# Expert matmuls in two column halves, the second one with weights as stationary operand

## The chip, the cores and the metric

The kernel runs on one core of a Trainium2 chip. The metric is device time in microseconds (us) of one execution. A core has TensorE (PE, matmul; PEld is its weight load), VectorE (DVE), ScalarE (ACT), GpSimd (POOL), SyncE (SP, which here only issues transfers) and 16 DMA engines. TensorE reads from SBUF and writes to PSUM, whose banks VectorE and ScalarE empty.

## The reference

A small vision tower on 32 images of 3x96x96: 36 tokens per image, 1152 tokens of 128 features. It makes shifted patch tokens, a rotary attention block with a feed-forward net, a lower-triangular token mix, a differential attention block, and last a block with attention and a mixture of 64 experts. The change touches the experts only:

```python
ef = gate_i.reshape(-1)              # two experts of 64 for each token
pos = ...                            # place of the token in its expert's list
keep = (pos < C)                     # C = 2 * (T * 2 // E) = 72 slots
buf = jnp.zeros((E, C, H)).at[ef, posc].add(tok)
h = jax.nn.gelu(jnp.einsum('ech,ehf->ecf', buf, w1) + b1[:, None, :])
y = jnp.einsum('ecf,efh->ech', h, w2) + b2[:, None, :]
ys = y[ef, posc] * (gf * keep)[:, None]
return x + ys.reshape(T, TOP_K, H).sum(axis=1)
```

Here E is 64, C is 72, H is 128 and F is 512, so each expert has two weight matrices of 128x512 and 512x128 float32, 512 KB together.

## The kernel before

The first two thirds of the program are the blocks ahead of the experts; their order on each engine is a table written out by hand (ORDERS_FOUND), and nothing of it changes. The tokens are then written to a table of slots in HBM (`slot_rows`), and from there come back as `xrows`, for each expert 72 rows on 72 partitions, with the row's target and its gate in two more columns.

The expert part is a loop over e, 0 to 63, written separately for each engine, with a lag (LAG = 2) between the first and the second matmul of an expert. For expert e:

- TensorE turns the 72x128 rows to 128x72 (`x_turn`, L1005, into bank 2 or 3), two steps ahead; VectorE scales and shifts them into `xe` (`x_in_place`, L1435).
- First matmul: for each of FC = 4 chunks c of 128 hidden features, the weights 128x128 from `ring` are stationary and `xe` (128x72) moves. The result, 128x72, goes to one of three rotating parts of `scores`, the name of four PSUM banks.
- ScalarE applies the gelu with the bias, four instructions of 128x72 (L1063), into `hT`.
- Second matmul, for expert f = e - 2: `hT` (128x72) is stationary and the weights (128x128) move, four chunks accumulating into 72x128 in bank 0 or 1. TensorE's program interleaves it with the first matmul of e, chunk by chunk.
- VectorE multiplies the result by the gate into `ys`, 72x128 (L1461), one of NY = 8 buffers. GpSimd sends the rows of `ys` to their places in HBM (`expert_rows`) by an indirect DMA (L754), here called a scatter.
- The weights sit in `ring`, RING = 11 slots of one expert each. SyncE refills the slot of expert e - 11 with expert e by one 512 KB transfer (L608), once `ys_ready` says that the old expert is through.

After the last scatter SyncE brings `expert_rows` back, VectorE adds the two rows of each token, and the sum is stored.

Every float32 matmul in the program stands as two MATMUL records in the trace, each with its own LDWEIGHTS; a turn stands as one. A record named `128*72 128x128` has 128 rows and 72 columns of stationary operand and 128 moving columns. One older part of the kernel already uses parts of the array: `weigh` multiplies 128x32 pieces, whose results go to partitions 0, 32, 64 and 96 in turn (records `128*32 128x36`), and `score` multiplies 32x36 pieces of four row groups, with results at partitions 0 and 64 (records `32*36 32x72`).

## Time and profile before

| what | value |
|---|---|
| median of 3 runs | 422.57 us (422.13 to 425.06) |
| profiled execution: span of its instructions | 420.9 us |
| mean granted TensorE clock | 0.844 of full speed |
| PE busy / PEld busy | 329.6 us (78%) / 283.9 us (67%) |
| DVE / ACT / POOL busy | 233.6 / 223.2 / 200.1 us |
| expert part | about 295 to 409 us, then about 12 us to the end |

The span reaches from the first to the last instruction of one profiled execution; the median lies 1.7 us above it. A busy share is an average over stages with different limits, so the expert part has to be read by itself. An engine can be idle and still be late: what counts is which wait ends last.

### The profile page before, as it was taken

Reading aid. Unit: us, or ns where it says so; the run is one execution under the profiler, and the core shown is the slowest. Engines: PE = TensorE matmul, PEld = TensorE weight load, DVE = VectorE, ACT = ScalarE, POOL = GpSimd, SP = SyncE. Lnnn points to the kernel's source line nnn. Section 1 sums busy time; section 2 is a strip of 40 time slices with the busy share of each in tenths; the row PEclk is TensorE's granted clock in tenths of the full one; section 3 lists DMA queues with packets and bytes.
Section 4 is the critical chain, followed back from the end, with each engine's and each line's share of the span. In section 5 each row is a group of like instructions: output and inputs, shape, how many; then the busy total and the mean of one; then the engine's idle time right before and its main releaser. Section 6 shows DMA issues by size and latency. Waiting matters only on the chain.

```text
span 420.9 us, 10393 instructions
## 1 busy us (share of the span) xinstructions
PE 329.6 (78%) x3936; PEld 283.9 (67%) x3936; DVE 233.6 (56%) x615; ACT 223.2 (53%) x640; POOL 200.1 (48%) x312
## 2 busy tenths in 40 slices
PE   8858767888859558876978666369999899999960
PEld 6646556776546446654767545259999899999950
DVE  1475886744397967887558675453333333333324
ACT  2346657776686645585476743300454555555530
POOL 3177586568640131622214656562255455555550
PEclk9998999999688765596689856557999999999995
DMA  8999903000000000000000000004789898999406
GB/s 280 374 404 258 116 21 96 2 2 1 2 2 2 2 2 2 0 4 0 3 2 2 11 19 18 6 11 116 205 310 301 282 319 318 321 314 316 142 12 168
DMA packets 21235, 50.14 MB, mean 119 GB/s; under 512 B 4116, under 2 KB 10340, under 8 KB 21058
## 3 DMA queue, kind: packets, MB, share of 16 engines
q1 hardware_dynamic: 18146, 46.96, 35.3%
q0 software_dynamic: 3040, 2.52, 2.2%
q8 instruction: 32, 0.52, 0.5%
q14 instruction: 17, 0.14, 0.1%
HBM read 43.97 MB, written 7.72 MB: 123 GB/s over the span
## 4 chain that ended last, share of the span: by engine, by line
PE 56%; DVE 16%; ACT 11%; POOL 6%; issue 5%; DMA 3%; SPq 1%; another core or an unknown queue 0%; POOLq 0%; DVEq 0%
PE bank L762 35%; PE scores L762 17%; ACT work L1063 5%; DVE mx L1292 3%; DVE work L1301 2%; DVE stats L1229 2%; POOL rstd L647 2%; DMA work<-in_patches 2%; ACT norm L1063 2%; PE bank L771 1%; PE bank L837 1%; ACT src L1063 1%; ACT xT L1063 1%; PE bank L1005 1%; DVE sm L1310 1%
## 5 line engine op out<-in xcount | busy, mean ns | idle before, releaser
L1063 ACT ACTIVATE work<-scores,b1T 128x72 f32<-128x72 f32 x256 | 61.2, 322 | 69.9 <-PE scores L762 65.9
L762 PE MATMUL bank<-ring,work 128*72 128x128 f32 x512 | 97.2, 274 | 0.0
L762 PE MATMUL scores<-work,ring 128*128 128x72 f32 x512 | 89.1, 258 | 1.3 <-DVE work L1435 1.1
L754 POOL DMA_INDIRECT expert_rows<-work,put_u x64 | 59.8, 935 | 63.0 <-issue 43.6
L762 PEld LDWEIGHTS scores<-work,ring 128*128 128x128 f32 x512 | 76.9, 191 | 1.7 <-DVE work L1435 1.2
L1063 ACT ACTIVATE work<-bank 128x288 f32<-128x288 f32 (+2 forms) x136 | 47.4, 375 | 52.4 <-PE bank L762 35.0
L1461 DVE TENSOR_SCALAR work<-bank,work 72x128 f32<-72x128 f32 x64 | 22.2, 347 | 70.5 <-issue 46.8
L762 PEld LDWEIGHTS bank<-ring,work 128*72 128x72 f32 x512 | 53.8, 145 | 0.2 <-ACT work L1063 0.2
L645 POOL TENSOR_SCALAR rstd<-mv 96x3 f32<-96x3 f32 x32 | 9.5, 296 | 71.2 <-DVE mv L1232 70.1
L762 PE MATMUL bank<-xTp,wT 128*128 128x288 f32 x80 | 36.6, 614 | 4.5 <-ACT xTp L1063 2.6
L762 PE MATMUL bank<-wT,xTp 128*128 128x128 f32 x192 | 29.4, 317 | 2.7 <-ACT work L1063 2.7
L724 POOL DMA_INDIRECT slot_rows<-xrow,flat_u x24 | 25.1, 1048 | 13.1 <-issue 7.5
L762 PEld LDWEIGHTS bank<-xTp,wT 128*128 128x128 f32 x80 | 21.4, 289 | 14.5 <-ACT xTp L1063 5.2
L762 PEld LDWEIGHTS bank<-wT,xTp 128*128 128x128 f32 x192 | 28.1, 230 | 3.6 <-issue 3.0
L647 POOL TENSOR_TENSOR rstd<-rstd,minus_half 96x3 f32<-96x3 f32 x32 | 28.2, 882 | 2.7
L1292 DVE TENSOR_REDUCE mx<-scores 100x32 f32<-100x1152 f32 x16 | 21.5, 1345 | 10.5 <-PE scores L762 10.4
L1435 DVE TENSOR_SCALAR work<-bank,cols 128x72 f32<-128x72 f32 x64 | 21.7, 341 | 9.0 <-PE bank L1005 8.8
L837 PE MATMUL bank<-cst,work 100*128 100x100 f32 x192 | 21.9, 273 | 4.0 <-DVE work L1325 3.1
L762 PE MATMUL scores<-work 32*36 32x72 f32 x1024 | 16.9, 258 | 10.1 <-DVE work L1301 4.9
L762 PEld LDWEIGHTS scores<-work 32*36 32x36 f32 x1024 | 13.5, 122 | 15.2 <-issue 13.5
L837 PEld LDWEIGHTS bank<-cst,work 100*128 100x128 f32 x192 | 19.7, 156 | 5.9 <-DVE work L1325 3.8
L1063 ACT ACTIVATE work<-work 100x1152 f32<-100x1152 f32 (+1 forms) x20 | 20.3, 1014 | 5.7 <-DVE work L1301 5.6
(157 smaller groups left out, 611.5 us busy)
## 6 DMA issues: line engine op xcount, KB each, us to landing
ring<-in_experts SPq DMA_DIRECT2D x64, 512.0 KB
work<-in_patches SPq DMA_DIRECT2D x3, 864.0 KB, 10.9
slot_rows<-hid SPq DMA_DIRECT2D x1, 2340.0 KB, 30.7
work<-slot_rows SPq DMA_DIRECT2D x7, 292.5 KB
wT<-in_weights SPq DMA_DIRECT2D x1, 1664.0 KB, 14.5
expert_rows<-mid POOLq DMA_DIRECT2D x2, 576.0 KB, 5.1
ring<-expert_rows SPq DMA_DIRECT2D x4, 288.0 KB, 4.3
expert_rows<-work,put_u POOLq DMA_INDIRECT x64
```

The lines of the kernel that those rows point to most:

```text
L645: st.step(pool.tensor_scalar(n, m, -1.0, None, ALU.mult))
L647: st.link(pool.tensor_tensor(r, r, minus_half[0:TP, 0:TPB], ALU.pow))
L724: pool.indirect_dma_start(out=xslot[:, :], out_offset=bass.IndirectOffsetOnAxis(ap=flat_u[:, TPB * b + n, k:k + 1], axis=0), in_=xrow[:, b ...
L754: pool.indirect_dma_start(out=ytok[:, :], out_offset=bass.IndirectOffsetOnAxis(ap=put_u[:, e:e + 1], axis=0), in_=ys[0:CAP, e % NY, :], in ...
L762: return nc.tensor.matmul(o, a, b, start=start, stop=stop)
L837: last = nc.tensor.transpose(o[:, SROWS * q:SROWS * (q + 1)], probs[0:SROWS, n % 2, q, p, :, :].rearrange("p a k -> p (a k)"), const("iden ...
L1063: return nc.scalar.activation(o, i, f, **kw)
L1229: st.step(v.bn_stats(stats[:, u, i, :], source(i)))
L1292: st.link(v.tensor_reduce(m3, sc, AX_X, ALU.max))
L1301: v.tensor_tensor(e4, sc, m3.unsqueeze(3).broadcast_to([SROWS, QUADS, 2 * PAIRS, SEQ]), ALU.subtract).then_inc(S["exp_in"], 1)
L1435: v.tensor_scalar(xe[:, e % NX, :], banks[i][:, 0:CAP], col("L1_ffn_ln2_g"), col("L1_ffn_ln2_b"), ALU.mult, ALU.add).then_inc(S["xe_ready" ...
L1461: v.tensor_scalar(ys[0:CAP, f % NY, :], banks[f % 2][0:CAP, 0:D], xrows[0:CAP, f, D + 1:D + 2], None, ALU.mult).then_inc(S["ys_ready"], 1)
```

## The change

Both matmuls of an expert are written in halves of PART = 64 output rows, with output at PSUM partitions 0 and 64. In the second one the operands change places: the weights, 128x64 for each half and chunk, are stationary and `hT` (72 columns) moves, so the result is 128x72, features by slots, and no longer 72x128. VectorE therefore copies it to a new buffer `yT` (L1482 in the changed kernel), TensorE turns it back into `scores` bank 3 two steps later (`y_turn`, L1018, YLAG = 2), and VectorE scales it from there into `ys` (L1475). The loop has two more steps at its end. The chunks of the two matmuls are no longer interleaved: all of the first, then all of the second. The refill of a ring slot waits for `y_full` in place of `ys_ready`.

```diff
+YLAG = 2
+PART = 64
+        yT = third.take([NX, CAP])
...
             for e in range(RING, E):
                 s = e % RING
-                sp.wait_ge(S["ys_ready"], e - RING + 1)
+                sp.wait_ge(S["y_full"], e - RING + 1)
...
+            def y_turn(g):
+
+                pe.wait_ge(S["yT_ready"], g + 1)
+                if g == 0:
+                    pe.wait_ge(S["bias_added"], NB)
+                else:
+                    pe.wait_ge(S["ys_ready"], g)
+                nc.tensor.transpose(scores[0:CAP, 3, 0:D], yT[:, g % NX, :], const("ident")).then_inc(S["y_turned"], 1)
...
-            for e in range(E + LAG):
+            for e in range(E + LAG + YLAG):
                 if e + 2 < E:
                     x_turn(e + 2)
                 f = e - LAG
+                if f >= YLAG:
+                    y_turn(f - YLAG)
...
-                if f >= 0:
+                    for c in range(FC):
+                        for u in range(0, D, PART):
+                            last = mm(scores[u:u + PART, e % 3, CAP * c:CAP * c + CAP], ring[:, e % RING, D * c + u:D * c + u + PART],
+                                      xe[:, e % NX, :])
+                    last.then_inc(S["h_in"], 1)
+                if 0 <= f < E:
                     pe.wait_ge(S["h_full"], f + 1)
                     pe.wait_ge(S["bias_added"], min(f + 1, 2))
                     if f >= 2:
-                        pe.wait_ge(S["ys_ready"], f - 1)
-                for c in range(FC):
-                    if e < E:
-                        last = mm(scores[:, e % 3, CAP * c:CAP * c + CAP], ring[:, e % RING, D * c:D * c + D], xe[:, e % NX, :])
-                        if c == FC - 1:
-                            last.then_inc(S["h_in"], 1)
-                    if f >= 0:
-                        last = mm(banks[f % 2][0:CAP, 0:D], hT[:, f % NX, c, :], ring[:, f % RING, FF + D * c:FF + D * c + D],
-                                  start=(c == 0), stop=(c == FC - 1))
-                        if c == FC - 1:
-                            last.then_inc(S["y_full"], 1)
+                        pe.wait_ge(S["yT_ready"], f - 1)
+                    for c in range(FC):
+                        for u in range(0, D, PART):
+                            last = mm(banks[f % 2][u:u + PART, 0:CAP], ring[:, f % RING, FF + D * c + u:FF + D * c + u + PART],
+                                      hT[:, f % NX, c, :], start=(c == 0), stop=(c == FC - 1))
+                    last.then_inc(S["y_full"], 1)
...
+                g = e - LAG - YLAG
+                if g >= 0:
+                    if g >= NY:
+                        dve.wait_ge(ys_gone[g % NY], 16 * (g // NY))
+                    dve.wait_ge(S["y_turned"], g + 1)
+                    v.tensor_scalar(ys[0:CAP, g % NY, :], scores[0:CAP, 3, 0:D], xrows[0:CAP, g, D + 1:D + 2], None, ALU.mult
+                                    ).then_inc(S["ys_ready"], 1)
                 f = e - LAG
-                if f >= 0:
-                    if f >= NY:
-                        dve.wait_ge(ys_gone[f % NY], 16 * (f // NY))
+                if 0 <= f < E:
                     dve.wait_ge(S["y_full"], f + 1)
-                    v.tensor_scalar(ys[0:CAP, f % NY, :], banks[f % 2][0:CAP, 0:D], xrows[0:CAP, f, D + 1:D + 2], None, ALU.mult
-                                    ).then_inc(S["ys_ready"], 1)
+                    if f >= NX:
+                        dve.wait_ge(S["y_turned"], f - NX + 1)
+                    v.tensor_copy(yT[:, f % NX, :], banks[f % 2][:, 0:CAP]).then_inc(S["yT_ready"], 1)
```

TensorE's program before, in the middle of the expert part, from the last matmul of one step into the next (output rows x moving columns; a row is a matmul, `cst,work` a turn):

```order
L762 MATMUL bank1<-ring,work 72x128
L1005 MATMUL bank2<-cst,work 128x72 [waits xe_ready,rows_here2]
L762 MATMUL scores<-work,ring 128x72 [waits h_full,bias_added,ys_ready,expert_here8,xe_ready]
L762 MATMUL bank0<-ring,work 72x128
L762 MATMUL scores<-work,ring 128x72
```

TensorE's program for one whole step of the changed kernel and the turn that begins the next:

```order
L1008 MATMUL bank2<-cst,work 128x72 [waits xe_ready,rows_here8]
L1018 MATMUL scores<-cst,work 72x128 [waits ys_ready,yT_ready]
L765 MATMUL scores<-work,ring 64x72 [waits h_full,expert_here5,xe_ready]
L765 MATMUL scores<-work,ring 64x72 x7
L765 MATMUL bank0<-work,ring 64x72 [waits yT_ready,bias_added,h_full]
L765 MATMUL bank0<-work,ring 64x72 x7
L1008 MATMUL bank3<-cst,work 128x72 [waits xe_ready,rows_here8]
```

Where a turn, four first and four second matmuls in alternation made a step, two turns, a run of eight half matmuls and another run of eight make one now. Every matmul of these runs has 72 moving columns.

VectorE's program before, where a chunk of rows begins:

```order
L1435 TENSOR_SCALAR work<-bank2,cols 128x72 [waits bank2_full,h_in]
L1455 CAST put_u<-work 72x8 [waits rows_here5]
L1461 TENSOR_SCALAR work<-bank0,work 72x128 [waits y_full,ys_gone6]
L1435 TENSOR_SCALAR work<-bank3,cols 128x72 [waits bank3_full,h_in]
L1461 TENSOR_SCALAR work<-bank1,work 72x128 [waits y_full,ys_gone7]
```

and VectorE at the same place in the changed kernel:

```order
L1449 TENSOR_SCALAR work<-bank2,cols 128x72 [waits bank2_full,h_in]
L1469 CAST put_u<-work 72x8 [waits rows_here5]
L1475 TENSOR_SCALAR work<-scores,work 72x128 [waits y_turned,ys_gone4]
L1482 COPY work<-bank0 128x72 [waits y_turned,y_full]
L1449 TENSOR_SCALAR work<-bank3,cols 128x72 [waits bank3_full,h_in]
```

VectorE has one instruction more in each step, and the scaling of an expert stands ahead of the copy of the expert two places later. TensorE's last steps in the changed kernel, after the last first matmul, are:

```order
L1018 MATMUL scores<-cst,work 72x128 [waits ys_ready,yT_ready]
L765 MATMUL bank0<-work,ring 64x72 [waits yT_ready,bias_added,h_full]
L765 MATMUL bank0<-work,ring 64x72 x7
L1018 MATMUL scores<-cst,work 72x128 [waits ys_ready,yT_ready]
L765 MATMUL bank1<-work,ring 64x72 [waits yT_ready,bias_added,h_full]
L765 MATMUL bank1<-work,ring 64x72 x7
L1018 MATMUL scores<-cst,work 72x128 [waits ys_ready,yT_ready] x2
```

Before, only the two second matmuls stood there. Now four turns are spread among and behind them, each waiting for VectorE.

## Rows read from the trace of the kernel before

**Rows 1.** The page: engine totals; the granted clock in forty slices, tenths.
```profile
PE 329.6 (78%) x3936; PEld 283.9 (67%) x3936; DVE 233.6 (56%) x615; ACT 223.2 (53%) x640; POOL 200.1 (48%) x312
...
PEclk9998999999688765596689856557999999999995
```

**Rows 2.** The page: the chain that ended last, by line.
```profile
PE bank L762 35%; PE scores L762 17%; ACT work L1063 5%; DVE mx L1292 3%; DVE work L1301 2%; DVE stats L1229 2%; POOL rstd L647 2%; DMA work<-in_patches 2%; ACT norm L1063 2%; PE bank L771 1%; PE bank L837 1%; ACT src L1063 1%; ACT xT L1063 1%; PE bank L1005 1%; DVE sm L1310 1%
```

**Rows 3.** Windows; after the engines: PEclk, DMA share, GB/s.
```profile
302.00:320.00 18.00, 18.00 (x182) 18.00 (x182) 6.29 (x22) 9.76 (x41) 9.57 (x11) 1.00 0.86 300
320.00:340.00 20.00, 18.92 (x189) 18.67 (x187) 6.74 (x24) 10.41 (x44) 10.18 (x12) 1.00 0.91 296
...
360.00:390.00 30.00, 30.00 (x303) 30.00 (x300) 10.90 (x38) 16.94 (x71) 16.68 (x18) 1.00 0.91 316
```

**Rows 4.** Timeline, TensorE, one expert step: start, length, engine, form, count.
```profile
345.16 0.23 PE L1005 MATMUL bank<-cst,work 72*128 72x72 f32 x1
345.23 0.38 PE L762 MATMUL scores<-work,ring 128*128 128x72 f32 x2
345.45 0.38 PE L762 MATMUL bank<-ring,work 128*72 128x128 f32 x2
345.67 0.34 PE L762 MATMUL scores<-work,ring 128*128 128x72 f32 x2
...
346.86 0.23 PE L1005 MATMUL bank<-cst,work 72*128 72x72 f32 x1
```

**Rows 5.** Timeline, TensorE, a job in 32-column parts.
```profile
214.73 0.28 PE L762 MATMUL bank<-wT,xTp 128*128 128x128 f32 x1
214.94 0.77 PE L762 MATMUL bank<-work 128*32 128x36 f32 x64
```

**Rows 6.** Timeline, TensorE, a scores job.
```profile
180.59 0.89 PE L762 MATMUL scores<-work 32*36 32x72 f32 x64
```

**Rows 7.** Timeline, TensorE, the last piece of a scores job and what follows.
```profile
72.31 0.22 PE L762 MATMUL scores<-work 32*36 32x72 f32 x1
72.47 0.46 PE L762 MATMUL bank<-wT,hid 128*96 128x128 f32 x2
```

**Rows 8.** Windows around the jobs of 5 and 6; PEclk is third last.
```profile
180.50:181.50 1.00, 1.00 (x67) 0.80 (x66) 0.97 (x4) 0.95 (x4) 0.00 (x0) 1.00 0.07 16
214.00:216.00 2.00, 1.97 (x76) 1.75 (x75) 1.52 (x3) 1.94 (x7) 0.00 (x0) 1.00 0.00 0
```

**Rows 9.** Groups of instructions, 302 to 400 us.
```profile
L1063 ACT ACTIVATE work<-scores,b1T 128x72 f32<-128x72 f32 x227 | 54.4, 322 | 43.9 <-PE scores L762 39.9 <-PE bank L762 2.4 <-issue 1.6
L754 POOL DMA_INDIRECT expert_rows<-work,put_u x57 | 53.3, 935 | 45.1 <-issue 41.1 <-DVE work L1461 4.0
...
L1461 DVE TENSOR_SCALAR work<-bank,work 72x128 f32<-72x128 f32 x57 | 19.8, 347 | 62.9 <-issue 44.1 <-PE bank L762 18.8
L1435 DVE TENSOR_SCALAR work<-bank,cols 128x72 f32<-128x72 f32 x57 | 19.4, 340 | 0.3
```

**Rows 10.** Timeline, TensorE, the first expert steps.
```profile
295.55 1.08 PE L762 MATMUL scores<-work,ring 128*128 128x72 f32 x8
...
297.89 0.41 PE L762 MATMUL scores<-work,ring 128*128 128x72 f32 x2 [0.23 <-ACT work L1063]
```

**Rows 11.** The chain of waits, end: start, length, what.
```profile
404.42 1.09 PE bank L762 x10
...
406.72 0.36 DVE work L1461
...
408.47 2.01 DMA expert_rows<-work,put_u
```

**Rows 12.** Timeline, GpSimd, the last scatters.
```profile
407.23 0.93 POOL L754 DMA_INDIRECT expert_rows<-work,put_u  x1 [0.30 <-DVE work L1461]
408.47 0.94 POOL L754 DMA_INDIRECT expert_rows<-work,put_u  x1 [0.31 <-issue]
```

More of the change, by code:

```diff
@@ L471, in build @@
             probs_ready map_scaled ctx_ready gn_stat gn_back gn_ready out_added affine_ready hid_ready
-            mask_ready logits_ready picked run_ready slot_ready gate_in blank_made blank_sent put_ready xe_ready h_in h_full y_full ys_ready
+            mask_ready logits_ready picked run_ready slot_ready gate_in blank_made blank_sent put_ready xe_ready h_in h_full y_full yT_ready y_turned ys_ready
             x2_ready h_summed src_ready stored rope_q_ready mixed rows_doubled gm_ready gm_turned gmT_ready bias_full bias_added lam_ready square_ready pT_ready gn_mean_back gn_centred
@@ L1448, in _ @@
             x_in_place(1)
-            for e in range(E + LAG):
+            for e in range(E + LAG + YLAG):
                 if e + 2 < E:
```

## The prediction

> **What bounds the kernel now.** I read the engine totals first and they decide little: TensorE is busy for 78% of the span and no engine for all of it [rows 1]. The chain that ended last tells more: 35% and 17% of the span lie on the two matmul lines `bank` and `scores` of L762 [rows 2], which in the expert part are the second and the first matmul. So I took windows of that part. From 302 to 390 us TensorE has work in its queue at all times but for 1.1 us (18.92 of 20 in the second row), at a granted clock of 1.00, the 2.4 GHz level; the DMA engines have a share of 0.86 to 0.91 [rows 3]. One step of the loop, from one turn of rows to the next, takes 346.86 - 345.16 = 1.70 us [rows 4]. Against this stand, per step, 54.4 / 57 = 0.95 us of ScalarE, 0.935 of GpSimd, 0.347 + 0.340 of VectorE [rows 9]. So TensorE sets the pace, with the DMA engines close behind: 0.91 x 1.70 = 1.55 us of each step. From the first whole step (297.89 [rows 10]) to the end of the last one (404.42 [rows 11]) there are 62 steps, 62 x 1.70 + 1.1 = 106.5 us. Whatever a step gains counts 62 times; what comes after is a tail of 404.42 to 408.47, the last scatter's start [rows 11, 12], and then some 12 us that nobody touches.
>
> **The step of the changed kernel.** Removed: four first matmuls of 128x128 by 72 and four second of 128x72 by 128, two records each, in all 1.60 us of the step (the turn has the rest). Added: 16 half matmuls, 32 records, all with 72 moving columns, and a turn with 128. What 32 records cost depends on whether the halves that write partitions 0 to 63 and 64 to 127 run at the same time.
>
> The nearest rows: the job of 64 records `128*32 128x36` takes 0.77 us from first start to last end [rows 5] at a granted clock of 1.00 [rows 8]. A single record lasts about 0.22 us [rows 7], so the starts spread over 0.55 us: 0.0087 us a record, 0.035 for a round of four 32-column parts. A piece with 36 moving columns cannot take less than half of what 72 columns take, and 72 columns take 0.07 us (turn to first matmul, 345.16 to 345.23 [rows 4]). So 0.035 is the time of one piece: the four column parts ran together, loads included. The job of 64 records `32*36 32x72` has eight positions in the array, 8 rounds with 72 moving columns: (0.89 - 0.22) / 8 = 0.083 us a round [rows 6, 8], with the start-up of the job in it.
>
> For 128x64 pieces a round is two records, so the step has 16 rounds, 15 intervals between the first and the last. At 0.065 to 0.07 us (the stream of 72 columns) they cost 1.0 us, at 0.083 they cost 1.25. I take 0.065, since a step has no job start inside, and the stream sets the round if the parts overlap: 15 x 0.065 = 0.98.
>
> Then the changes of shape, two in each step. From full array to column parts: 214.73 to 214.94, 0.21 us with 128 moving columns ahead [rows 5], which fits the new turn ahead of the first half matmul. From parts back to the full array, after 72 columns: 72.31 to 72.47, 0.15 us [rows 7]. Between the two turns, 0.07 us [rows 4]. Sum of the step: 0.98 + 0.15 + 0.07 + 0.21 = 1.41, I take **1.40 us**; bounds 1.35 and, at 0.083 a round, 1.25 + 0.43 = 1.68. Gain 62 x 0.30 = **18.6 us**. What the switch costs is in these rows already. The Trainium skill ("TensorEngine Tiling (Array Packing)", Key Properties) says that changing the tiling mode drains TensorE; the trace agrees, 0.21 us where 0.11 separates two full matmuls with 128 moving columns (345.45 to 345.67 is two of them [rows 4]).
>
> **What else moves.** VectorE gets a copy of 128x72 out of a bank; the nearest row is L1435, 0.340 us of the same shape [rows 9]. The sum is 1.03 us of a 1.40 us step: hidden, at no cost, and if VectorE were late it would be late for a turn that stands a whole step behind its copy. ScalarE's 0.95 us fit too. GpSimd needs 1.24 us from scatter to scatter when they follow closely (407.23 to 408.47 [rows 12]), so it fits 1.40 with 0.16 to spare: it costs nothing, but is next in line. The `ys_gone`, `yT_ready` and `y_turned` waits all point at least one step back.
>
> The refill of the ring now waits for `y_full`; that starts it about 0.4 us earlier, which counts only if transfers bind. Do they? One expert takes 1.55 us of all 16 engines in the 360 to 390 row (0.91 x 1.70), 0.86 x 1.70 = 1.46 in the 302 to 320 row, and 0.91 x 20 / 11.1 steps = 1.64 in the 320 to 340 row [rows 3]. That is more than a step of 1.40. But 11 experts are in SBUF at the start, so only 53 have to come. The first slot is free when step 2 ends, 297.5 + 1.4 = 298.9, and I allow 1.3 us until its data flow: from 300.2 on, they are in by 300.2 + 53 x 1.55 = 382.4. TensorE wants the last at 297.5 + 61 x 1.40 + 0.4 = 383.3. A tie by 0.9 us; with irregular arrivals I charge **0.5 us** (bounds 0 and, at 1.64, 3.8).
>
> At the head, steps 0 and 1 have first matmuls alone, eight records in 1.08 and about 1.0 us, and step 2 waited 0.23 us for ScalarE [rows 10] ahead of both matmuls, now only ahead of the second. Gain 0.4 us (0 to 1.2).
>
> At the tail, the last expert's result must be copied (0.34), turned (0.28 with hand-over) and scaled, each turn waiting for the scaling ahead of it, and the scatters follow each other at 1.24 us. Before it was 408.47 - 404.42 = 4.05 us from the last whole step to the last scatter [rows 11, 12]; I reckon 5.3, a loss of **1.25 us** (0.8 to 2.5).
>
> **Sum.** -18.6 - 0.4 + 0.5 + 1.25 = -17.25. The profiled span is 420.9, 1.7 below the median 422.57; I keep that distance: 403.6 of span, **405.3 us** of time. The bounds of the terms give 401 to 409 for this case, where the round stays below about 0.07.
>
> **Rivals.**
>
> *The transfers set the pace.* If DMA can't go beyond what the 320 to 340 row shows, or a fuller queue makes the share useless, the last expert is late by 3.8 us at 1.64 and by 7 us at 1.70 (316 GB/s as now): 408 to 413. For it: shares of 0.86 to 0.91 already [rows 3]. Against: a share below 1 is room, and the ring holds 11. Chance 0.10.
>
> *The round is 0.083, not 0.065.* Then a step is 1.68, the gain 1.2, and 420.9 to 422.8 comes out: no change. Against: that value has a job's start in it. Chance 0.04.
>
> *The halves take turns.* With no overlap there are 31 intervals of 0.065: 2.02 + 0.43 = 2.45 us a step, 62 x 0.75 = 46 us more, 470. It decides at 1.27 us for the 32 records, 0.041 each: above it the change loses. Rows 5 show 0.0087 a record, but for 32-column parts; nothing there shows 64-column parts with 128 rows. Chance 0.06.
>
> *TensorE can't take in so many records.* A step has 34 MATMUL records in place of 17; above 1.70 / 34 = 0.050 us a record the kernel gets slower. At twice the 0.012 us a record of the 64-record job (0.77 / 64 [rows 5]) it is 0.8 us, hidden below 1.40, and only at more than four times it would show: 0.06 gives 2.04 a step, 443 us. Chance 0.02. The Trainium skill ("TensorE: Matmul & The Clock Gate", Back-to-back issue gap) gives about 62 ns per MATMUL in one decode setting, as a bound where the array work is shorter; by it, estimated, the step would be 34 x 0.062 = 2.1 us and the kernel some 25 us slower. The trace disagrees: 0.012 us a record.
>
> *The clock falls.* Now TensorE keeps 1.00 through the expert part [rows 1, 3]. With two drains in a step and perhaps waits for weights it might be granted 1.2 GHz for stretches: at that level a step is 2.8 us, so each step spent there loses 1.1 against now; it outweighs the gain if more than a fifth of the steps run so (0.30 x 4/5 against 1.1 / 5), and all of them give 490. Against: both kinds of jobs with parts keep 1.00 [rows 8]. Chance 0.03.
>
> **How the numbers follow.** The forecast has 0.75, and with the transfers' case 0.85 lie in 401 to 413, which is my range; the slow cases are far outside and are left out. A measurement of this kernel tells a change from none at about 1%, 4 us. Faster by more: 0.75 + 0.10 + a quarter of the round's case = 0.86. Within 1%: 0.03. Slower: 0.06 + 0.02 + 0.03 = 0.11.
>
> **What the profile after should show.** Steps of about 1.40 us between turns of rows; 16 records of the first matmul within 0.5 us; gaps of 0.21 and 0.15 us at the changes of shape; granted clock 1.00; the DMA share at 0.97 or more; the last scatter at about 391 us. A step of 1.55 with a DMA share near 1 and TensorE waiting for `ring` is the transfers' case. A step of 1.68 with no waits is the round's; 2.4 is the halves in turn. I would also be wrong if GpSimd needed more than 1.40 for a scatter while more transfers are under way, since everything hangs on `ys_gone` after eight experts.

## The result: 453 us in the first runs, 412 to 418 us on other chips

The changed kernel took 453.12 us (median of 4 runs, 451.93 to 453.69) where the kernel before took 423.26 (4 runs): a ratio of 1.071, 95% interval 1.067 to 1.075. The forecast was 405.3. It was slower by 7%, and the profile below shows how.

That is half of the result. The same kernel, unaltered, ran again beside the experiments on three other chips. There it took 417.81 once beside 417.6 of the kernel before (13 runs), 412.12 beside 415.55 (one run each), and 412.8 (5 runs) beside 419.28 (7 runs), a ratio of 0.984 (0.980 to 0.988). Only the last pair can carry a difference: on that same chip a single run of the kernel before had taken 414.71 earlier, so 3 to 6 us between single runs say nothing. So there are two questions: what costs 30 us in the first runs, and what makes more than 405 of it where that cost is absent.

**The profile after, first runs.** The page: engine totals, granted clock, DMA share, the chain that ended last, and four groups (mean ns of one behind the comma, then idle time before it and its releaser).

```profile
PE 333.7 (74%) x5024; PEld 263.4 (58%) x5024; DVE 243.1 (54%) x679; ACT 222.7 (49%) x640; POOL 199.8 (44%) x312
...
PEclk9988999998878656867895665699999999999985
DMA  8999430000000000000000000377767677765005
...
PE 31%; another core or an unknown queue 20%; DVE 20%; ACT 10%; issue 8%; POOL 6%; DMA 3%; SPq 1%; DVEq 0%; POOLq 0%
...
L1077 ACT ACTIVATE work<-scores,b1T 128x72 f32<-128x72 f32 x256 | 60.9, 321 | 97.7 <-PE scores L765 95.6
L757 POOL DMA_INDIRECT expert_rows<-work,put_u x64 | 59.8, 935 | 94.5 <-DVE work L1475 84.8
...
L1482 DVE COPY work<-bank 128x72 f32<-128x72 f32 x64 | 14.5, 227 | 88.4 <-remote 84.2
...
L1475 DVE TENSOR_SCALAR work<-scores,work 72x128 f32<-72x128 f32 x64 | 21.9, 342 | 4.3 <-PE scores L1018 1.4
```

Nothing has become slower by itself: ScalarE's activation 321 ns, the scatter 935 and the scaling 342 are the durations of [rows 9], and the new copy takes 227 ns. The clock in the expert part is at 9 of 10 or more, as in [rows 1]. But a fifth of the chain is "another core or an unknown queue", on a kernel that has one core, and VectorE's copy waits 84.2 us for something "remote". Windows of the expert part, as [rows 3]:

```profile
302.00:320.00 18.00, 14.60 (x291) 11.45 (x286) 6.17 (x26) 7.80 (x33) 7.44 (x9) 1.00 0.70 248
320.00:340.00 20.00, 16.43 (x316) 12.62 (x311) 6.84 (x28) 8.86 (x39) 8.68 (x10) 1.00 0.72 246
360.00:390.00 30.00, 24.56 (x470) 19.02 (x467) 10.45 (x44) 13.45 (x56) 12.75 (x14) 1.00 0.73 244
```

Every engine is idle more than before, the DMA engines too (0.70 to 0.73 in place of 0.86 to 0.91): no engine and no queue is the bound, something makes all of them wait. TensorE's timeline shows it, one good step and one bad one, beside [rows 4]:

```profile
344.33 0.28 PE L1008 MATMUL bank<-cst,work 72*128 72x72 f32 x1
344.45 0.27 PE L1018 MATMUL scores<-cst,work 128*72 128x128 f32 x1
344.65 0.72 PE L765 MATMUL scores<-work,ring 128*64 128x72 f32 x16
345.20 0.30 PE L765 MATMUL bank<-work,ring 128*64 128x72 f32 x4
345.72 0.38 PE L765 MATMUL bank<-work,ring 128*64 128x72 f32 x5 [0.22 <-issue]
346.47 0.47 PE L765 MATMUL bank<-work,ring 128*64 128x72 f32 x7 [0.37 <-issue]
346.87 0.28 PE L1008 MATMUL bank<-cst,work 72*128 72x72 f32 x1
347.41 0.28 PE L1018 MATMUL scores<-cst,work 128*72 128x128 f32 x1 [0.26 <-DVE work L1482]
347.62 0.72 PE L765 MATMUL scores<-work,ring 128*64 128x72 f32 x16
348.17 0.67 PE L765 MATMUL bank<-work,ring 128*64 128x72 f32 x16
348.77 0.28 PE L1008 MATMUL bank<-cst,work 72*128 72x72 f32 x1
```

The step from 346.87 to 348.77 is 1.90 us, the one ahead of it 2.54; 4.45 us for two, all along, from about the eighth step on. In the bad one TensorE stops twice in the middle of a run of half matmuls, waiting for "issue" alone, so for none of its operands. VectorE meanwhile, in the same stretch:

```profile
343.36 0.35 DVE L1475 TENSOR_SCALAR work<-scores,work 72x128 f32<-72x128 f32 x1
346.52 0.23 DVE L1482 COPY work<-bank 128x72 f32<-128x72 f32 x1 [2.81 <-remote]
```

That copy needs the second matmul whose last record, by the records, ended at 344.40. The semaphore update of that record (semaphores are the counters by which the engines wait for each other) stands in the trace at 346.49. Those of the two turns behind it (ends 344.61 and 344.72) stand at 346.53 and 346.56, that of the first matmul, which ended at 345.37, at 346.72; in the good step each comes 0.01 to 0.02 us after its end. So for 2.1 us no update of TensorE arrives, while its matmul records go on, with two stops. I call this a **hold**. It comes every 4.45 us, and each turn back and each scatter then is late too.

The kernel before has the same thing once in its trace, and I had not looked for it. VectorE and ScalarE, there:

```profile
326.93 0.35 DVE L1461 TENSOR_SCALAR work<-bank,work 72x128 f32<-72x128 f32 x1 [2.57 <-PE bank L762]
326.87 0.96 ACT L1063 ACTIVATE work<-scores,b1T 128x72 f32<-128x72 f32 x4 [2.39 <-PE bank L762]
```

TensorE's records there are gapless (324.79 to 326.88), and three of its updates, of records that ended at 325.12, 325.35 and 325.41, stand together at 326.79 to 326.86. One step of 2.97 us follows, the only one in that trace that is longer by more than 0.2 us, the first five aside.

One thing more sets these traces apart. A part of their semaphore records is missing. The changed kernel has 4259 of them here and 4800 to 4807 in its three traces on other chips. In the kernel before, from 310 to 390 us, only 73 of the 138 updates that TensorE makes are on record; in the changed kernel, with its holds, 142 of 146.

### The profile page after: what moved, and what is told of

It reads as the page before. It is cut to its first block, busy times and chain, and to the rows that moved or that the text cites. A ratio compares the mean times of both kernels' runs of the same rounds, so it can differ in the third digit from the quotient of the medians.

```text
span 451.7 us, 12697 instructions
## 1 busy us (share of the span) xinstructions
PE 333.7 (74%) x5024; PEld 263.4 (58%) x5024; DVE 243.1 (54%) x679; ACT 222.7 (49%) x640; POOL 199.8 (44%) x312
## 4 chain that ended last, share of the span: by engine, by line
PE 31%; another core or an unknown queue 20%; DVE 20%; ACT 10%; issue 8%; POOL 6%; DMA 3%; SPq 1%; DVEq 0%; POOLq 0%
PE bank L765 21%; PE scores L765 6%; ACT work L1077 4%; DVE work L1475 3%; DVE mx L1306 2%; DVE work L1315 2%; DVE stats L1243 2%; POOL rstd L650 2%; DMA work<-in_patches 2%; ACT norm L1077 2%; PE scores L1018 2%; DVE work L1449 1%; DVE work L1482 1%; PE bank L774 1%
## 5 line engine op out<-in xcount | busy, mean ns | idle before, releaser
L765 PE MATMUL bank<-work,ring 128*64 128x72 f32 x1024 | 57.0, 230 | 16.9 <-issue 16.9
L1482 DVE COPY work<-bank 128x72 f32<-128x72 f32 x64 | 14.5, 227 | 88.4 <-remote 84.2
L765 PEld LDWEIGHTS bank<-work,ring 128*64 128x64 f32 x1024 | 43.4, 136 | 24.7 <-issue 24.5
L765 PE MATMUL scores<-work,ring 128*64 128x72 f32 x1024 | 46.1, 232 | 0.0
L765 PEld LDWEIGHTS scores<-work,ring 128*64 128x64 f32 x1024 | 36.7, 136 | 8.8 <-issue 0.6
L727 POOL DMA_INDIRECT slot_rows<-xrow,flat_u x24 | 25.1, 1046 | 13.0 <-issue 7.5
L1306 DVE TENSOR_REDUCE mx<-scores 100x32 f32<-100x1152 f32 x16 | 21.5, 1345 | 10.6 <-PE scores L765 10.4
L1018 PE MATMUL scores<-cst,work 128*72 128x128 f32 x64 | 17.7, 277 | 11.6 <-DVE work L1482 7.7
L1475 DVE TENSOR_SCALAR work<-scores,work 72x128 f32<-72x128 f32 x64 | 21.9, 342 | 4.3 <-PE scores L1018 1.4
```

The source lines that it names most:

```text
L727: pool.indirect_dma_start(out=xslot[:, :], out_offset=bass.IndirectOffsetOnAxis(ap=flat_u[:, TPB * b + n, k:k + 1], axis=0), in_=xrow[:, b ...
L765: return nc.tensor.matmul(o, a, b, start=start, stop=stop)
L1018: nc.tensor.transpose(scores[0:CAP, 3, 0:D], yT[:, g % NX, :], const("ident")).then_inc(S["y_turned"], 1)
L1306: st.link(v.tensor_reduce(m3, sc, AX_X, ALU.max))
L1475: v.tensor_scalar(ys[0:CAP, g % NY, :], scores[0:CAP, 3, 0:D], xrows[0:CAP, g, D + 1:D + 2], None, ALU.mult).then_inc(S["ys_ready"], 1)
L1482: v.tensor_copy(yT[:, f % NX, :], banks[f % 2][:, 0:CAP]).then_inc(S["yT_ready"], 1)
```

## The experiments

Eighteen runs in five groups; those of one group ran on one chip, and groups two and five on the same one, so that three chips stand beside that of group one. A time is that of a single execution where no interval is given. Steps are counted from one turn of rows to the next, and a mean step is that of steps 10 to 60.

**Group one: what makes the step long?**

The supply of instructions by itself. Ahead of the experts of the kernel before stand 1024 MATMUL records of half matmuls and 1024 of quarter ones:

```diff
+            for n in range(512):
+                u = 64 * (n % 2)
+                mm(scores[u:u + 64, 0, 0:72], wT[:, 0, u:u + 64], wT[:, 1, 0:72])
+            stay_awake(HEAD_WARM)
+            for n in range(512):
+                u = 32 * (n % 4)
+                mm(scores[u:u + 32, 0, 0:72], wT[:, 0, u:u + 32], wT[:, 1, 0:72])
```

> The kernel before, with two long runs of matmuls put in ahead of the experts, while no weights are on their way: 512 half matmuls of 128x64 by 72 moving columns (1024 records), and 512 quarter matmuls of 128x32 by 72 (1024 records). Their results are not used. Theory A (TensorE can be fed only so many records in the long run: 34 in 2.22 us of the changed kernel's step, 0.065 us each, and faster only until a store of instructions is empty): both runs begin at 0.031 or less a record and then fall to about 0.065 a record whatever the shape, so each takes some 60 to 67 us and the kernel about 545 us. Theory B (what holds TensorE up in the changed kernel is the traffic of weights) and theory C (it is the waits among the engines): the halves stay at 0.031 us a record (32 us) and the quarters at 0.017 (17 us), and the kernel takes about 472 us.

```profile
336.95 2.21 PE L762 MATMUL scores<-wT 128*32 128x72 f32 x128 [1.43 <-issue]
340.68 2.21 PE L762 MATMUL scores<-wT 128*32 128x72 f32 x128 [1.52 <-issue]
```

493.02 us. The halves ran at 31.6 ns a record, 32 us long, with one gap of 0.28 us: theory A, a limit by the count of records near 0.065 us, is out. The quarters ran 128 records in 2.0 us and then stopped, for "issue" again; 128 records with their weight loads are 256 instructions, and such stretches begin 3.73 to 4.00 us apart, from the first full one on. In that time one packet of 16 KB comes on the DMA queue of instructions. So with a DMA share of 0.02 TensorE is given 256 instructions in some 3.7 us, and halves are just within it (4.0).

No traffic of weights, in the changed kernel (its experts from 11 on use the weights that lie in the slots, and TensorE waits for no refill):

```diff
                 sp.wait_ge(S["y_full"], e - RING + 1)
-                sp.dma_start(ring[:, s, :], ins["experts"][e]).then_inc(w_here[s], 16)
+                pass
```

> The changed kernel without the 53 refills of the ring: experts 11 to 63 use the weights left in the slots, so the output is wrong from there on; all matmuls and waits else stay. Theory A (feeding by record count): the step stays at 2.2 us, the kernel at 450 us or a little less. Theory B (traffic of weights holds TensorE up): the step falls to about 1.4 us, the kernel to about 400 us. Theory C (waits among the engines): the step stays at 2.2 us.

456.87 us, mean step 2.26, the holds as before, so the traffic of weights (theory B) does not make them. The windows, with a DMA share of 0.03:

```profile
320.00:340.00 20.00, 16.13 (x307) 12.55 (x307) 6.93 (x30) 8.62 (x38) 8.40 (x9) 1.00 0.03 6
```

The change without halves, then only the halves of the first matmul:

```diff
-PART = 64
+PART = 128
```

> The changed kernel with parts of 128 output rows, so no halves and no change of shape in the array, but the second matmul still swapped, copied and turned back; 18 records in a step in place of 34. The array needs 16 x 0.111 (a load of 128 columns each) + 0.2 = 2.0 us a step. Theory A: 18 x 0.065 = 1.2 us is less than that, so the step is 2.0 us with no hold-ups, the kernel 441 us, faster than with halves. Theory C (the waits of the longer way over copy and turn cost): steps of two lengths in turn and semaphores that come late, 2.2 us or more, 450 us.

```diff
+                if e < E:
+                    for c in range(FC):
+                        for u in (0, 64):
+                            last = mm(scores[u:u + 64, e % 3, CAP * c:CAP * c + CAP], ring[:, e % RING, D * c + u:D * c + u + 64], xe[:, e % NX, :])
+                    last.then_inc(S["h_in"], 1)
                 for c in range(FC):
-                    if e < E:
-                        last = mm(scores[:, e % 3, CAP * c:CAP * c + CAP], ring[:, e % RING, D * c:D * c + D], xe[:, e % NX, :])
-                        if c == FC - 1:
-                            last.then_inc(S["h_in"], 1)
```

> The kernel before with the first matmul in halves of 64 rows, all four chunks ahead of the second matmul, which stays whole and unswapped: 16 + 8 + 1 = 25 records in a step. The array needs 8 x 0.062 + 0.21 + 8 x 0.111 + 0.15 = 1.74 us. Theory A: 25 x 0.065 = 1.63 us lies just below the array's time, so the step is about 1.75 us with a few hold-ups, the kernel about 426 us. Theory C: no copy and no turn, so no late semaphores at all, 1.74 us.

Whole swap: 436.94 us, every step from step 6 on 1.92 or 1.91, no hold; the copy, the turn back and their waits do no harm at this length of step. First halves: 437.00, 1.74 a step up to step 23, then two long steps in every five. The waits there name the same "remote":

```profile
ACT work L1064 <- remote: 23.4, 7, 3.4
...
DVE work L1462 <- remote: 20.3, 8, 2.8
```

So holds seemed to go with halves (or with short records, or with changes of shape). All of group one ran on a single chip.

**Group two: changes of shape, semaphores, the hand-over.**

```diff
-                nc.tensor.transpose(banks[2 + e % 2][:, 0:CAP], xrows[0:CAP, e, 0:D], const("ident")[0:CAP, 0:CAP]
-                                    ).then_inc(bank_full[2 + e % 2], 1)
+                for u in range(0, D, PART):
+                    last = mm(banks[2 + e % 2][u:u + PART, 0:CAP], xrows[0:CAP, e, u:u + PART], const("ident")[0:CAP, 0:CAP])
+                last.then_inc(bank_full[2 + e % 2], 1)
```

This edit and the like one for the turn back (with the copy ahead of it widened to 128 columns) make `one shape`; this edit on the kernel before makes `turn halves`:

> The changed kernel with both turns also written in halves of 64 output rows, as full float32 matmuls with the identity (the copy before the second turn is widened to 128 columns, the added ones zero). TensorE then never changes shape in the expert part, and a step has 40 MATMUL records in place of 34. Theory C (the two changes of shape in each step make TensorE hold back its semaphore updates and stall): no holds, a step of about 1.4 us (20 rounds of 0.065, and 0.07), about 404 us. Theory D (TensorE is handed instructions slower than a step of 34 to 40 records at the array's pace needs, whatever their shape): holds remain, a step of at least the 2.23 us of the changed kernel, scaled with the records 2.6 us, 453 to 478 us.

> The kernel before, in which only the turn of the rows is written in two halves of 64 output rows (four MATMUL records in place of one): 20 records a step and two changes of shape a step, everything else as before. By the array alone the step is 1.70 + 0.13 (a second round) + 0.21 - 0.11 + 0.15 - 0.07 = about 2.0 us, some 439 us. Theory C: holds of TensorE's semaphore updates of about 2 us come as in the changed kernel, and VectorE waits in the remote way for tens of us; above 445 us. Theory D: no holds at 20 records in 2.0 us, about 439 us.

TensorE's part of the step alone, 24 times in each of three runs, in the kernel before (the inner lines; `waits` are on semaphores that are full already):

```diff
+                    a = nc.tensor.transpose(scores[:, 1, 0:CAP], wT[0:CAP, 0, :], const("ident")[0:CAP, 0:CAP])
+                    c = nc.tensor.transpose(scores[0:CAP, 2, 0:D], wT[:, 1, 0:CAP], const("ident"))
+                    for half in range(2):
+                        for m in range(FC):
+                            for u in (0, 64):
+                                last = mm(o, wT[:, m, u:u + 64], wT[:, 4, 0:CAP], start=(half == 0 or m == 0), stop=(half == 0 or m == FC - 1))
```

> The kernel before, with three runs of 24 steps of TensorE's part of the changed kernel's step put ahead of the experts, on data that stand ready: two turns, then 16 and 16 half records (34 records a step), with no transfers of weights and no work of other engines. The first run has no semaphores, the second has the four increments of a step, the third also waits that are met already. 12 full matmuls stand between the runs. Theory C: stalls in all three runs (step 2.2 us in the mean in place of 1.41). Theory D, if it is the supply of instructions alone: the first steps at 1.41 us, then stalls in all three, bounded by what long runs showed, 128 records in 3.7 to 4.0 us, that is 1.0 us for 34 records, so no stalls: all three runs at 1.41 us. Theory E (increments or waits each take time of TensorE's sequencer, and with 34 short records too little is left): the first run at 1.41, the second or the third with stalls, up to 2.2 us a step.

The changed kernel without copy and turn back (the lines of the turn back and of its scaling fall away with them, and the output is incomplete):

```diff
-                    v.tensor_copy(yT[:, f % NX, :], banks[f % 2][:, 0:CAP]).then_inc(S["yT_ready"], 1)
+                    v.tensor_scalar(ys[0:CAP, f % NY, 0:CAP], banks[f % 2][0:CAP, 0:CAP], xrows[0:CAP, f, D + 1:D + 2], None, ALU.mult
+                                    ).then_inc(S["ys_ready"], 1)
```

> The changed kernel without what follows the second matmul: both matmuls in halves and the second with its weights stationary, but its result (features by slots) is not copied and not turned back. VectorE scales a 72x72 part of it straight into the buffer of rows, so the scattered rows are incomplete and the output is not the reference's. 33 records and two changes of shape a step, one semaphore hand-over less. Theory C and D both keep the holds (a step of 2.1 to 2.3 us, 445 to 455 us). If the hand-over by the copy and the turn back is what makes the holds: a step of 1.4 us, about 404 us.

None of the four had a hold. One shape: 410.91 us. Turn halves: 440.80, a step of 2.06, against some 2.0 as priced. Without turning back: 408.25. The steps alone: 1.47 in all three runs, against 1.41 as expected, so neither their increments nor waits that are met already cost anything here. The kernel before took 414.71 on this chip and 420.36 on that of group one. That no theory fitted, and that all were without holds at once, made the chip a suspect.

In `one shape` TensorE had another kind of stall: every 122 or 244 MATMUL records, up to 2.2 us long, from step 8 until the weights were nearly all in (122 with as many weight loads and the semaphore events are 256 instructions, though I saw that only later).

**Group three: the unaltered kernel again.**

> The changed kernel once more, unaltered, beside the next three on one chip, since the kernel before took 420.4 us beside the first four runs and 414.7 beside the last four. If the holds belong to the kernel: 445 to 453 us, steps of 2.2 us in the mean. If they belong to the chip or to the run: steps of 1.4 to 1.5 us and about 405 us, as the run without turning back showed (408).

> The version without changes of shape (both turns in halves, 40 records a step) against the kernel before, timed. One look gave 410.9 against 414.7. Theory: its steps are 1.35 us by the array, and what it loses are stalls every 256 instructions of TensorE, one for each fetch of instructions, while the weights are under way. Expected a ratio of 0.97 to 0.995 and the same stalls, 0.3 to 2.2 us each, some 16 of them, ending when the weights are in.

> The changed kernel with the turn of the rows alone written in halves (four records in place of one); the turn back stays one record on the whole array. 37 records a step, still two changes of shape a step. Theory G (the turn back as one whole-array record, between its copy and its scaling, makes the holds): holds, at least the changed kernel's 2.2 us a step, 445 us or more. Theory H (the holds need changes of shape around the turn of the rows): none, about 1.37 + 0.21 = 1.6 us a step, 412 to 418 us.

> The changed kernel with the turn back alone written in halves (with the copy ahead of it widened to 128 columns, the added ones zero); the turn of the rows stays one record on the whole array. 37 records a step, two changes of shape a step. Theory G: no holds, about 1.6 us a step, 412 to 418 us. Theory H, or any that goes by the two changes of shape with 34 records or more: holds, 445 us or more.

The changed kernel: 417.81, with no hold. One shape, timed: 418.08 against 417.6, ratio 0.999 (0.995 to 1.003), no difference, outside the 0.97 to 0.995 that I had expected. Rows' turn in halves 417.58, turn back in halves 418.47, both without holds, so that pair tells nothing of holds; both theories G and H fall with the control. In the trace of the changed kernel the steps are 1.47 us, but for a stall in every seventh or so: at 315.8, 327.4, 339.9, 351.0, 362.9, 374.6 and 387.3 us, 0.6 to 2.2 us each (one more stands at 304.4, and up to step 24 there are shorter ones of 0.2 to 0.7 us halfway between). From 315.8 to 327.4 TensorE took 242 MATMUL, 242 LDWEIGHTS and 30 semaphore events, from 327.4 to 339.9 it took 241, 240 and 29: 510 to 514 instructions, two packets of 16 KB.

**Group four: are the stalls late instructions?**

> The changed kernel unaltered, as the control for the next three on the same chip. Theory J (holds go with the chip or the run, not with the kernel alone): either about 418 us with steps of 1.47 us and a stall every 512 instructions, or about 453 us with holds in every second step, nothing between. Which of the two it is decides how the next three are read.

> The changed kernel without the refills of the ring (experts from 11 on use stale weights, so the output is not the reference's): no weight traffic in the expert part. Theory K (the stalls every 512 instructions are fetches of instructions that come late because the weight transfers fill the DMA engines): no stalls, every step 1.47 us, about 405 us where the control shows 418. Theory L (the fetch is late by itself when TensorE eats 256 instructions in 5.2 us): the stalls stay, about 418. Where the control has holds: 456 us as on the first chip.

> The kernel before with three runs of 24 of TensorE's steps alone. On the chip of the first look it had steps of 1.47 us without holds in all three. Where the control has no holds: the same. Where it has holds, this tells what they need: with theory M (the holds are TensorE's own way of working through short records with increments and waits on that chip) the runs with increments or waits show 2.2 us a step; with theory N (they need other engines at work on PSUM or real waits) 1.47 in all three.

> Long runs of half and quarter matmuls by themselves, DMA idle, as in the first experiment, where 256 instructions came in 3.7 to 4.0 us at best. If the supply of instructions is the same on chips without holds: the same numbers, 31.2 ns a record for halves and a stall every 128 records for quarters, 493 us. If chips differ in the supply: on one without holds 256 instructions in less than 3.5 us.

Control 412.12, no holds, mean step 1.675, with one of its stalls here:

```profile
352.29 0.48 PE L765 MATMUL bank<-work,ring 128*64 128x72 f32 x9
353.56 0.47 PE L765 MATMUL bank<-work,ring 128*64 128x72 f32 x7 [0.79 <-issue]
```

The packet of instructions ahead of it was on the DMA engines from 351.24 to 352.21, and TensorE went on 1.35 us later; in the long runs it is 1.3 to 1.5 us from a packet's end to the restart. Without refills: 404.62, and every one of steps 6 to 62 is 1.47 or 1.48 us, TensorE busy without a gap:

```profile
320.00:340.00 20.00, 20.00 (x462) 16.90 (x460) 11.70 (x44) 13.05 (x56) 12.47 (x14) 1.00 0.05 10
```

This is the very kernel that took 456.87 in group one: 462 records in these 20 us, 307 there. Theory K holds in this: the stalls go when the weights' traffic goes, all of them. A packet of instructions takes no longer on the DMA engines with the traffic (0.97 us in the median from 300 to 385 us) than without (1.18), so it is late before its transfer begins; what keeps it there, the queue, the engines or the memory, no run tells apart. The steps alone were 1.47 again:

```profile
330.00:365.00 35.00, 35.00 (x799) 29.65 (x800) 0.00 (x0) 0.00 (x0) 0.00 (x0) 1.00 0.01 3
```

The long runs: 485.22 us, and the stretches of quarters again 3.73 us apart in four of six cases (4.00 and 3.46 in the others), so the supply is about the same on both chips and is not what makes the holds. The other end of that run is telling: the experts of the kernel before, behind it, have all steps from the sixth on at 1.70 here, while in group one they had steps of 1.82, 1.76, 1.75 and 2.91, as the trace that I predicted from had 1.82 and 2.97. And the trace there has 3534 semaphore records, this one of the same program 4762.

**Group five: timing, and fewer weights in flight.**

> The changed kernel unaltered, timed against the kernel before. Without holds: a ratio of 0.990 to 1.000 (steps of 1.47 us, some ten stalls of 0.3 to 2.2 us from late instruction fetches, a mean step of 1.67 us against 1.70 before). With holds as in the first runs: 1.07.

```diff
                 sp.wait_ge(S["y_full"], e - RING + 1)
+                if e >= RING + 2:
+                    sp.wait_ge(w_here[(e - 2) % RING], 16 * ((e - 2) // RING + 1))
```

> The changed kernel, in which SyncE issues the transfer of expert e only when that of expert e - 2 has landed, so that no more than two of 512 KB are in flight in place of about three. Theory K (the fetch of instructions waits behind the weights that are queued): the stalls every 512 instructions become rarer or shorter, below half their sum of some 9 us. What it may cost: two transfers in flight may not fill the DMA engines; if an expert then takes 1.8 us, TensorE waits for ring at the end, up to 8 us. So 405 to 420 us. If the stalls stay as long while the transfers are thinned, the fetch is late for another reason than the queue of weights. With holds on this chip: about 450, and the comparison says nothing of the stalls.

The changed kernel: 412.8 against 419.28, ratio 0.984 (0.980 to 0.988). The trace is of the slowest of its five runs, 416.7; it does not show where the others are 4 us shorter. Its longest stall shows a second cost:

```profile
332.13 0.23 PE L765 MATMUL bank<-work,ring 128*64 128x72 f32 x1
334.62 0.72 PE L765 MATMUL bank<-work,ring 128*64 128x72 f32 x15 [2.27 <-issue]
...
336.24 1.18 PE L765 MATMUL bank<-work,ring 128*64 128x72 f32 x16
```

```profile
334.00:336.00 2.00, 1.38 (x29) 1.15 (x30) 0.57 (x3) 0.00 (x0) 0.09 (x1) 1.00 0.67 259
336.00:338.00 2.00, 2.00 (x31) 1.57 (x28) 0.66 (x4) 0.96 (x4) 0.83 (x1) 0.51 0.81 263
```

TensorE had 2.27 us without work, up to 334.62; from 336 us on the granted clock is 0.51, the 1.2 GHz level, and it is back at 1.00 by 340: the steps from 331.3 on are 4.02, 2.08 and 2.41. Two in flight: 439.85, ratio 1.051 (1.045 to 1.057). In steps 8 to 24, while the ring was still full, the stalls add up to 1.1 us where the unlimited kernel has 2.1, so thinner traffic did shorten them, in one trace. But the transfers fell behind:

```profile
302.00:320.00 18.00, 17.88 (x397) 14.90 (x395) 9.98 (x38) 11.41 (x48) 11.12 (x13) 1.00 0.78 235
```

235 GB/s are 2.2 us for an expert, against 332 in the same stretch of the unlimited kernel, and from step 25 on TensorE stops ahead of the first matmul in most steps (0.4 to 2.2 us), where it waits for `ring`: in the eleven of its 26 stops that I checked, it restarts 0.1 us after a transfer of weights has landed. My bound of 8 us for this, and the range of 405 to 420, were far too low; at two in flight the DMA share is 0.78, at about three 0.97.

## Why the prediction was wrong

**The array's part was right, but for 0.07 us a step.** The step of 1.40 was built of 15 rounds and three changes. In the trace after, first to second matmul is 0.55 us (344.65 to 345.20), the second one with the change back 0.60 (348.17 to 348.77), turn to turn 0.12, turn to first matmul 0.20: 1.47. A round is 0.062 to 0.069, against 0.065. What was off is the time between the two turns, 0.12 and not 0.07, and 0.02 in the rest: 0.07 a step, 4.3 us over 62. The halves run together, the clock stays at 1.00 in the steps themselves, GpSimd fits. The run without refills, where nothing else interferes, shows it whole: 89.27 us from the first turn of rows (291.23) to the last (380.50), against 103.54 for the kernel before on the same chip, a gain of 14.3. My terms for this stretch were 18.6 + 0.4; the 4.3 are the difference, within half a microsecond.

**The failed step is the rival on the intake of records**, to which I gave 0.02. It says: "At twice the 0.012 us a record of the 64-record job (0.77 / 64 [rows 5]) it is 0.8 us, hidden below 1.40". That is a burst of 64 records, 128 instructions. It says how fast TensorE works them off, and nothing of how fast the next ones come. In the long runs 256 instructions came in some 3.7 us. Before, a step has 38 instructions, and 256 last about 11 us. After, it has 72 and 256 last 5.2 us. That is 1.5 us of slack with idle DMA engines, and with the weights' transfers under way the slack is gone in about every second packet. Price: a mean step of 1.675 in place of 1.475, in all 99.65 - 89.27 = 10.4 us between the first and the last turn of rows (with refills and without, on one chip). With the 4.3 above, 14.7 of the 18.6 us that I had for the steps are lost. This is the loss on the chips without holds.

What is left agrees roughly with the measured gain: 103.54 (462.30 - 358.76, the experts of the kernel before behind the long runs) less 99.65 (388.16 - 288.51) is 3.9. From the last turn to the end it is 21.94 us after and 21.19 before, a loss of 0.75, which I had at 1.25. That makes 3.1 us, and the times on that chip differ by 3.4. (The first turn of rows stands at 288.5 to 294.4 us in the four traces of the changed kernel, the first runs' among them, so that the two times agree so closely is in part luck.)

**In the first runs the same step of the prediction fails, by more.** The sum 0.98 + 0.15 + 0.07 + 0.21 lets nothing but the array set the step, with 34 records as with 17. Measured was 2.23 us a step, 0.066 us a record, where the rival's own limit for a loss is 0.050. A step without holds and refills takes 1.475, and nearly all of the rest is the holds: without refills, so without the traffic that makes instructions late, it is 2.261 on the chip of group one. Why they come stays open, as said below.

**The second rival that I called away, transfers as the limit,** did not come in the form that I gave it. Without holds the DMA share is 0.87 to 0.97 from 302 to 360 us, and TensorE hardly waits for `ring`. Their harm is to the instructions. My charge of 0.5 us for transfers was the wrong term; the mechanism is another. That 412.12 and 412.8 lie inside the range of 401 to 413, and in the 408 to 413 of this rival, is luck.

**The clock's rival** (0.03) is there as a consequence, for two or three steps: in two of the changed kernel's three traces on other chips, behind a stall of 2.2 and one of 2.5 us from start to start, and with two transfers in flight behind waits of 1.4 and 1.7 us. The third had a stall of 2.0 us and kept 1.00.

**The holds** were in none of my cases. With refills the step is 2.230 - 1.675 = 0.56 us longer where they are, without refills 2.261 - 1.475 = 0.79, and they turn the sign. Between the two profiled executions, 451.7 and 420.9 us, 25.1 us lie between the first and the last turn of rows, 6.0 behind them, and -0.3 ahead. The Trainium skill's rule that I had weighed ("TensorE: Matmul & The Clock Gate", Back-to-back issue gap, about 62 ns per MATMUL) would give 2.1 us a step, near the 2.23 measured. The trace disagrees with it as the cause: the same 34 records take 1.47 us a step in three traces, and the half matmuls alone ran at 31.6 ns each on the chip of group one too.

**What stays open** is the cause of the holds. Shown: they come in the first runs and on the chip of group one (the changed kernel, the one without refills, the one with first halves; once in each of two traces of the kernel before), and in none of the 14 traces on three other chips, three of the unaltered kernel among them. Not needed for them: weights' traffic (the run without refills had them), a slower supply of instructions (equal in both long runs). Where they can come, they come more often with more and shorter records: once in some 60 steps in the kernel before (17 records a step), none with the whole swap (18, in a longer step), two steps in five with 25, every second step with 34. Whether the cause lies in the chip or in something else that the runs of a group share, no run here tells, nor whether TensorE's steps alone would show holds there, since that run fell on other chips both times.

**A rival that stands untested is the recording itself.** Every execution here was recorded (each has its span and its granted clock), and the six traces of the first runs and of group one are the very ones in which more than a few semaphore records are missing. From 310 to 390 us, of TensorE's updates 73 of 138 are there in the kernel before and 59 of 167 in the whole swap, where holds are rare or absent; in the changed kernel it is 142 of 146, and without refills 146 for 142, where holds are frequent. In the trace of first halves it turns within the trace: 21 of 30 from 302 to 320 us, ahead of the long steps, and 100 of 105 from 330 to 400, among them. On the other chips few are missing (168 of 168 are there from 310 to 380 in the changed kernel of group four; at the least it is 121 of 131, without turning back). That would fit a record of updates that either loses them or keeps TensorE back. It is not shown, and if it were so, an execution without recording might have no holds at all.

## What to carry to other kernels

Splitting matmuls to use the array better multiplies TensorE's instructions, and they have to be fetched. Count them: 256 in 11 us gave no such stall on the other chips, 256 in 5.2 us with the DMA engines near full gave stalls on "issue" in the middle of a run, however fast a short burst goes. A step shorter by 13% in the array, with nearly twice the instructions, gained 1.6% where it was timed on another chip and lost 7% in the first runs. And before an edit is credited or blamed, run the unaltered kernel again beside the variants: my first eight were read against a result that the next chips did not repeat. A single odd wait in the trace of before (2.57 us, once) was the first sign, and the missing semaphore records were the second: count the records of a trace against what the program makes.

## What the runs showed that I had not expected

- TensorE's semaphore updates can be held back for 2.1 us, while the records of its matmuls go on, and come together at the end of it; the profile calls the wait "remote" or "another core or an unknown queue" on a kernel with one core. The traces of the first runs and of group one lack a part of their semaphore records (11% of the changed kernel's, 26% of the long runs', by the same programs on other chips).
- Instructions come in packets of 16 KB, 256 each, most often 3.73 us apart (3.46 to 4.00) where TensorE waits for them; it restarts 1.3 to 1.5 us after a packet has landed.
- No refills: 404.62 us on one chip, 456.87 on another, for the same program, whose groups have the same durations (copy 233 and 227 ns, activation 321 and 321).
- Two transfers of 512 KB in flight move 235 to 241 GB/s, unlimited ones 312 to 332 (302 to 360 us).
